# Cross attention's last group projected as rows, batch by batch, over four residual tiles

## What is computed

```python
x = _layernorm(x + _L0_attn_ref(x, ...))
x = _layernorm(x + _L0_xattn_ref(x, ctx_2048, mask, Wq, bq, Wk, bk, Wv, bv, Wo, qn_w, kn_w))
x = _layernorm(x + _L0_ffn_ref(x, ...))
...
def _L0_xattn_ref(...):
    q = _rmsnorm((x @ Wq + bq) per head, qn_w)
    k, v = the same for ctx, 4 heads, each used by 4 query heads
    probs = softmax(q @ k.T / sqrt(128) + mask)
    return (probs @ v, heads side by side) @ Wo
```

## Time and profile before

| what | value |
|---|---|
| runs | 3067.51, 3069.43, 3078.80 us; median 3069.43 |
| profiled execution | 3078.59 us, of it 3076.8 us span of the core |
| busy in that span | TensorE 2767.8 us (90%), its weight loads 2474.5 (80%), VectorE 2054.7 (67%), ScalarE 1675.5 (54%), GpSimd 1762.0 (57%) |
| TensorE clock granted over the span | 0.949 of full speed |
| chain that ended last | TensorE 24% and GpSimd 8% of the span, VectorE 7% |

### The profile page before, as it was taken

How to read it: one execution, slowest core, us unless ns; L and a number is a source line. 1 busy time by engine, 2 the same in 40 slices (tenths; PEclk the granted TensorE clock), 3 DMA queues, 4 the chain that set the end, 5 groups by cost and what they waited for, 6 DMA issues and landing times. The chain is left out here.

```text
span 3076.8 us, 48615 instructions
## 1 busy us (share of the span) xinstructions
PE 2767.8 (90%) x16114; PEld 2474.5 (80%) x16114; DVE 2054.7 (67%) x4047; ACT 1675.5 (54%) x4244; POOL 1762.0 (57%) x2193
## 2 busy tenths in 40 slices
PE   8599999968999999986799789999999996879998
PEld 7488887857888888875799688888898885769998
DVE  5377777756878888886256466767677777774334
ACT  2155555536888888863455355655656553543222
POOL 0177777734766666663245278788888786540000
PEclk9699999988999999998899899999999998889999
DMA  5635555444332333231411321211211111532101
GB/s 205 198 103 160 152 156 159 152 149 146 120 114 94 111 115 115 85 122 54 127 50 56 112 84 64 79 55 56 78 64 60 57 41 58 181 124 88 33 27 33
DMA packets 215272, 310.81 MB, mean 101 GB/s; under 512 B 47190, under 2 KB 112770, under 8 KB 212914
## 3 DMA queue, kind: packets, MB, share of 16 engines
q1 hardware_dynamic: 215026, 307.70, 31.4%
HBM read 211.27 MB, written 96.37 MB: 100 GB/s over the span
## 5 line engine op out<-in xcount | busy, mean ns | idle before, releaser
L744 POOL TENSOR_TENSOR mh_quant_d<-mh_quant_a,mh_quant_d 128x512 f32<-128x512 f32 x208 | 277.4, 1334 | 17.4
L819 ACT ACTIVATE mh_quant_d<-mh_quant_d 128x512 f32<-128x512 f32 x256 | 159.8, 624 | 109.1 <-POOL mh_quant_d L744 108.8
L738 POOL TENSOR_SCALAR mh_quant_d<-mh_quant_a 128x512 f32<-128x512 f32 x208 | 132.8, 638 | 135.2 <-DVE mh_quant_err L722 89.4
L722 DVE TENSOR_REDUCE mh_quant_err<-mh_quant_d 128x8 f32<-128x512 f32 x256 | 173.4, 678 | 37.8 <-ACT mh_quant_d L819 36.1
L1580 PE MATMUL bank<-ga_eT,ga_v 128*128 128x400 f32 (+1 forms) x384 | 169.8, 524 | 30.3 <-DVE ga_zl L1766 30.2
L2277 POOL TENSOR_TENSOR fq_var<-fq_mv,eps_ln 100x1 f32<-100x1 f32 x16 | 3.7, 229 | 314.7 <-DVE fq_mv L2220 314.7
L1537 PE MATMUL bank<-ga_xt,ga_wqh 128*128 128x400 f32 x512 | 177.3, 409 | 1.6 <-DVE ga_xt L164 1.6
L1730 ACT ACTIVATE ga_e<-ga_e,ga_nm 100x361 f32<-100x361 f32 x256 | 152.8, 597 | 38.2 <-DVE ga_nm L1825 36.7
L777 POOL TENSOR_TENSOR ga_quant_d<-ga_quant_a,ga_quant_near 128x512 f32<-128x512 f32 x128 | 165.1, 1290 | 13.4 <-DVE ga_quant_err L722 2.9
L1726 ACT ACTIVATE ga_e<-ga_e,ga_rs 100x361 f32<-100x361 f32 x256 | 152.6, 596 | 18.2 <-DVE ga_rs L1807 18.2
L1853 POOL TENSOR_TENSOR ga_qrs<-ga_qms,minus_half 100x4 f32<-100x4 f32 x64 | 68.0, 1063 | 163.5 <-DVE ga_qms L1760 163.5
(11 more groups left out here) (435 smaller groups left out, 10495.7 us busy)
## 6 DMA issues: line engine op xcount, KB each, us to landing
keys_turned<-kv_kt SPq DMA_DIRECT2D x16, 1448.0 KB, 5.8
ga_kt<-keys_turned SPq DMA_DIRECT2D x64, 362.0 KB, 2.9
ga_xt<-x_turned SPq DMA_DIRECT2D x48, 400.0 KB, 4.9
mh_xt<-x_turned SPq DMA_DIRECT2D x48, 400.0 KB, 4.8
qkv<-m_rows SPq DMA_DIRECT2D x16, 1000.0 KB
kv_rows<-qkv SPq DMA_DIRECT2D x50, 320.0 KB, 3.3
raw<-x SPq DMA_DIRECT2D x64, 200.0 KB
kv_ctx<-in_ctx SPq DMA_DIRECT2D x32, 256.0 KB, 5.2
```

What stands on the lines that cost most here:

```text
L722: nc.vector.tensor_reduce(self.of(self.err, i)[:, s, :], self.error(i, s), AX, ALU.add).then_inc(self.summed.sem, 1)
L738: nc.gpsimd.tensor_scalar(e, a[:], 1.0 / SHRINKS[s], MAGIC, ALU.mult, ALU.add).then_inc(made.sem, 1)
L744: nc.gpsimd.tensor_tensor(e, a[:], e, ALU.subtract).then_inc(self.diff.sem, 1)
L819: nc.scalar.activation(self.error(i, s), self.error(i, s), ACT.Square).then_inc(self.squared.sem, 1)
```

## The change

`project_out`, the adds to `acc` and `turn_back` are no longer done for group 15. Instead `project_rows(j)`, in slots 252, 256, 260 and 264 on TensorE, makes the rows of batch j at once: four products of `acc` (what groups 3, 7 and 11 left there) with the identity, and 12 products with the 100 tokens standing and 512 columns of Wo moving, all into one bank of its own (`row_bank`: the two query banks, the projection's bank, a score bank). The tails 12 to 15 move to slots 263 to 266, and NT becomes 269. The residual tiles are four, two of them the tiles `x` that the phase no longer needs. SyncE loads four residuals in slot 208, and afterwards the residual of e + 4 three slots behind the tail e, ahead of that slot's store. On VectorE `add_rows(e)` now comes ahead of `normalise(e - 1)`, for all 16 tails.

```diff
-        NT = NU + 24
+        NT = NU + 13
+        RES = 4
...
-        res = [sb(f"{ph}_res{n}", [S, D], F32, ctx) for n in range(2)]
+
+        res = [sb(f"{ph}_res{n}", [S, D], F32, ctx) for n in range(2)] + x
...
-        for g in range(NG):
+        for g in range(NG - 1):
             at = 0
             for n, count in enumerate(y_counts):
                 y_slots[16 * (g + 1) + 8 + n] = (g, at, at + count)
                 at += count
-        y_done = {16 * (g + 1) + 8 + n: (g, f) for g in range(NG) for f, n in enumerate((4, 6, 7, 10))}
-        tails = {16 * (g + 2) + 3 + j: 4 * (g - (NG - BG)) + j for g in range(NG - BG, NG) for j in range(G)}
+        y_done = {16 * (g + 1) + 8 + n: (g, f) for g in range(NG - 1) for f, n in enumerate((4, 6, 7, 10))}
+        tails = {16 * (g + 2) + 3 + j: 4 * (g - (NG - BG)) + j for g in range(NG - BG, NG - 1) for j in range(G)}
+        first_row = 4 * (BG - 1)
+        tails.update({NU + 7 + j: first_row + j for j in range(G)})
+        rows_at = {NU - 4 + 4 * j: j for j in range(G)}
+        row_bank = q_bank + [y_bank, score_bank[0]]
...
                 if n == NU - 48:
-                    load_res(0)
-                    load_res(1)
+                    sp.wait_ge(x_turned.sem, x_turned.upto(15))
+                    for e in range(RES):
+                        load_res(e)
+                if n - 3 in tails and tails[n - 3] + RES < 16:
+                    e = tails[n - 3]
+                    sp.wait_ge(out_in[e % RES].sem, out_in[e % RES].upto(e // RES))
+                    load_res(e + RES)
                 if n - 1 in tails:
                     e = tails[n - 1]
-                    since(sp, normed, e)
-                    sp.dma_start(rows_of(xs[2], batch(NG - BG + e // 4, e % 4)), res[e % 2][:])\
-                        .then_inc(out_in[e % 2].sem, 16)
-                    if e + 2 < 16:
-                        since(sp, out_in[e % 2], e // 2)
-                        load_res(e + 2)
+                    sp.wait_ge(normed.sem, normed.upto(e))
+                    sp.dma_start(rows_of(xs[2], batch(NG - BG + e // 4, e % 4)), res[e % RES][:])\
+                        .then_inc(out_in[e % RES].sem, 16)
...
+            def project_rows(j):
+
+                g = NG - 1
+                pe.wait_ge(y_added.sem, y_added.upto(4 * (g - BG) + 3))
+                pe.wait_ge(z_lo.sem, z_lo.upto(4 * g + j))
+                if j < 2:
+                    pe.wait_ge(q_lo.sem, q_lo.upto(GH * NG - 1))
+                elif j == 2:
+                    pe.wait_ge(y_added.sem, y_added.upto(4 * (g - 1) + 3))
+                else:
+                    pe.wait_ge(masked.sem, masked.upto(NU - 1))
+                for f in range(KC):
+                    nc.tensor.matmul(row_bank[j][0:S, f * P:(f + 1) * P], acc[groups[g][1]][:, f, cols(j)], ident[:],
+                                     start=f == 0, stop=False, skip_group_check=True)
+                for hh in range(GH):
+                    last = mm3(row_bank[j][0:S, :], zh[g % 2][:, hh, cols(j)], zl[g % 2][:, hh, cols(j)],
+                               wo[0][:, hh, :], wo[1][:, hh, :], False, hh == GH - 1)
+                last.then_inc(rows_full.sem, 1)
...
-                if n in tails:
+                if n in tails and tails[n] < first_row:
                     turn_back(tails[n])
+                if n in rows_at:
+                    project_rows(rows_at[n])
...
             def add_rows(e):
-                k = e % 2
-                since(dve, tail_turned, e)
-                since(dve, res_in[k], e // 2)
-                nc.vector.tensor_tensor(res[k][:], tail_bank[0:S, :], res[k][:], ALU.add).then_inc(added.sem, 1)
+                k, r, from_ = e % 2, res[e % RES][:], tail_bank if e < first_row else row_bank[e - first_row]
+                if e < first_row:
+                    dve.wait_ge(tail_turned.sem, tail_turned.upto(e))
+                else:
+                    dve.wait_ge(rows_full.sem, rows_full.upto(e - first_row))
+                dve.wait_ge(res_in[e % RES].sem, res_in[e % RES].upto(e // RES))
+                nc.vector.tensor_tensor(r, from_[0:S, :], r, ALU.add).then_inc(added.sem, 1)
...
+                if n in tails:
+                    add_rows(tails[n])
                 if n - 1 in tails:
                     normalise(tails[n - 1])
-                if n in tails:
-                    add_rows(tails[n])
```

More of the change, by code:

```diff
@@ L1369, in cross_attention @@
         v_in = [Signal(f"{ph}_v_in{n}", len(range(n, NQ, 3)), 32) for n in range(3)]
-        res_in, out_in = ([Signal(f"{ph}_{c}{n}", 8, 16) for n in range(2)] for c in ("res_in", "out_in"))
+        res_in, out_in = ([Signal(f"{ph}_{c}{n}", 16 // RES, 16) for n in range(RES)] for c in ("res_in", "out_in"))
         made = Signal(f"{ph}_made", 4)
@@ L1380, in cross_attention @@
         attended, z_hi, z_lo = (Signal(f"{ph}_{c}", NQ) for c in ("attended", "z_hi", "z_lo"))
-        y_full, y_added = head("y_full"), head("y_added")
-        tail_turned, added, stats_made, mv_made, eps_added, rstd_made, normed = (
-            row16(c) for c in ("tail_turned", "added", "stats", "mv", "eps_added", "rstd", "normed"))
+        y_full, y_added = (Signal(f"{ph}_{c}", 4 * (NG - 1)) for c in ("y_full", "y_added"))
+        tail_turned, rows_full = Signal(f"{ph}_tail_turned", 4 * (BG - 1)), Signal(f"{ph}_rows_full", G)
+        added, stats_made, mv_made, eps_added, rstd_made, normed = (
+            row16(c) for c in ("added", "stats", "mv", "eps_added", "rstd", "normed"))
         kview = t["L0_xattn_Wq"].rearrange("(k p) n -> p k n", p=P)
@@ L1455, in load_res @@
             def load_res(e):
-                sp.dma_start(res[e % 2][:], rows_of(xs[1], batch(NG - BG + e // 4, e % 4))).then_inc(res_in[e % 2].sem, 16)
+                sp.dma_start(res[e % RES][:], rows_of(xs[1], batch(NG - BG + e // 4, e % 4))).then_inc(res_in[e % RES].sem, 16)
             load_x(0)
@@ L1771, in add_rows @@
             def add_rows(e):
-                k = e % 2
-                since(dve, tail_turned, e)
-                since(dve, res_in[k], e // 2)
-                nc.vector.tensor_tensor(res[k][:], tail_bank[0:S, :], res[k][:], ALU.add).then_inc(added.sem, 1)
-                since(dve, added, e)
-                nc.vector.bn_stats(stats[k][:], res[k][:]).then_inc(stats_made.sem, 1)
+                k, r, from_ = e % 2, res[e % RES][:], tail_bank if e < first_row else row_bank[e - first_row]
[5 more added lines that the diff above has]
+                nc.vector.tensor_tensor(r, from_[0:S, :], r, ALU.add).then_inc(added.sem, 1)
+                dve.wait_ge(added.sem, added.upto(e))
+                nc.vector.bn_stats(stats[k][:], r).then_inc(stats_made.sem, 1)
                 since(dve, stats_made, e)
@@ L1782, in normalise @@
             def normalise(e):
-                k = e % 2
-                since(dve, rstd_made, e)
-                nc.vector.tensor_scalar(res[k][:], res[k][:], mv[k][:, 0:1], rstd[k][:], ALU.subtract, ALU.mult)\
+                k, r = e % 2, res[e % RES][:]
+                dve.wait_ge(rstd_made.sem, rstd_made.upto(e))
+                nc.vector.tensor_scalar(r, r, mv[k][:, 0:1], rstd[k][:], ALU.subtract, ALU.mult)\
                     .then_inc(normed.sem, 1)
@@ L1877, in cross_attention @@
                       scored, masked, maxed, exped, recip, scaled, turned, copied, attended, z_hi, z_lo, y_full, y_added,
-                      tail_turned, added, stats_made, mv_made, eps_added, rstd_made, normed]):
+                      tail_turned, rows_full, added, stats_made, mv_made, eps_added, rstd_made, normed]):
             s_.hand_back()
```

## The result

| | before | after |
|---|---|---|
| median, us (7 runs each, same chip) | 3076.04 (3067.51 to 3079.65) | 3063.67 (3056.16 to 3071.45) |
| ratio of the times, 95% interval | | 0.9958 (0.9944 to 0.9972) |
| profiled execution: its time, its span, us | 3078.59, 3076.8 | 3056.16, 3054.4 |
| TensorE clock granted over the span | 0.949 | 0.955 |

So 0.42% less: by the ratio 12.9 us of 3076, with an interval of 8.6 to 17.2 us. That is inside the 0.5% that count as no change here, and the median lies in the predicted range of 3047 to 3065 us. The median of before moved from 3069.43 us in three runs to 3076.04 in seven, which is why the gain ends at 3063.67 and not near 3056.

What follows compares the result with a forecast made beforehand. Latency at the end of cross attention was taken as the bound. 9.9 us at the end, 2.3 of residual waits and 2.3 by the swapped order gave 14.5 us less: median 3069.43 to 3054.9 us, range 3047 to 3065.

Steps and rivals of the forecast that it cites:

- the end: End of cross attention: the last normalisation starts at 1460.0 where it was 1469.99, so 9.9 us less.
- rival B: Last group: residuals stay late, each of four adds waits 2.36 us, gain 7.1 us, 3062.3 us; chance 0.12.
- A row costs 3.8 us: One project_rows on TensorE: 2.77 us for 12 products plus 1.0 us for the identity passes.
- the 5.8 us: Three rows on TensorE's path: extra cost if 100-column weight loads were added to the products; gain then 8.7 us.
- Rows in slots 252 and 256 are paid in full: Last units on TensorE: rows of batches 0 and 1 are not hidden and cost 7.6 us.
- Rival A: Units' end: the rows in slots 252 and 256 are hidden, 22.1 us less, 3047.3 us; chance 0.12.
- `zl` starts 5.7 us later: VectorE after the last attended batch: the last `zl` starts at 1445.0 instead of 1439.36, delayed by the rows ahead.
- `zl` to the last normalisation 15.0 us: VectorE's last group: 13.0 us of work plus 2.0 us of residual waits, where it was 30.6 us.
- the loads' waits: Residual loads of tails 13 to 15: waits of 0.7, 1.1 and 0.2 us, together 2.0 us.
- Normalisation to the next load stays at 3.06 us: Phase end: last normalisation, store and its landing, up to the next phase's first load, keep their 3.06 us.
- 2.3 us of residual waits in tails 2 to 7, and 2.3 us by the swap: VectorE beside the units: waits go with four tiles; the swapped order takes 70% of 3.3 us excess in normalisations.
- Rival C: TensorE from slot 252 on: half clock makes it slower, at worst 16 us, 3085.6 us; chance 0.10.

Runs made afterwards that it cites:

- experiment 8: The whole change with only batch 0's row early, in slot 252, the other three in slots 262 to 264; ratio to the kernel before 0.9927.
- experiments 1 and 2: Kernel before with four residual tiles alone (ratio to before 0.9976), then also with add_rows(e) ahead of normalise(e - 1) (0.9958); neither has the rows.
- experiment 4: The whole change with all four rows behind the units, in slots 261 to 264; ratio to the kernel before 0.9937.
- experiments 9 and 10: Residual loads one slot earlier in SyncE's queue, four tiles: on the whole change (ratio to before 0.9959), then with all rows behind the units (0.9927).

## Why the prediction held, and where it did not

**The size.** 14.5 us were forecast with a range of 10 to 19 for that case; 13.5 were measured in the stretch and 12.9 (8.6 to 17.2) in the times. Two pieces of luck are in this. The stretch is near the sum because two misses offset each other: the end gave 8.0 us where 9.9 were forecast, and U gave 5.5 where 4.6 were, of which about 1.8 are the clock of before. Without that clock the stretch would have gained 11.7. And the level, 3063.67 us where 3054.9 was forecast, lies in the range by 1.3 us: from the median of 3069.43, 10 to 19 us less was 3050 to 3059, and only the part of the range that reached into rival B covered the 6.6 us by which the median of before moved.

By its own steps:

- *A row costs 3.8 us*: 3.61. The products were right (2.82 for 2.77), the identity passes took 0.79 where I took 1.0. The weight loads of 100 columns (0.17 us) stayed beside the products, so the 5.8 us that the prediction priced for loads that nothing hides did not come.
- *Rows in slots 252 and 256 are paid in full*: yes for the first, 3.63 us (experiment 8); the second was not moved alone. Rival A, that both are covered, is refuted: the three rows cost 8.1 us of E.
- *`zl` starts 5.7 us later*: E grew by 5.3 us.
- *`zl` to the last normalisation 15.0 us*: 16.70. The part without loads was 13.0 in the sum and 13.14 in the kernel with eight tiles. **The failed term is the loads' waits: 2.0 us predicted, 3.29 measured.** I priced each load by the one row of 2.86 us, which had no store just ahead of it (the next one was issued 0.54 us behind it). The loads of the changed kernel are issued 0.3 us behind a store and took 3.5 to 4.0 us. In the kernel with rows alone, where each load is issued once the store of its tile has landed, the five that an add waited for in the last two groups took 2.76 to 3.01 us. The sum said 0.7, 1.1 and 0.2 us of waiting for tails 13 to 15; it was 1.15, 1.52 and 0.62, each 0.4 to 0.5 more. Rival B, 9.4 us of such waits, was far off. The 2.5 us for 200 KB, an estimate by the Trainium skill's page "DMA: Bandwidth & Descriptors" ("Anatomy of one DMA"), whose section measured it on the path of DMAs that GpSimd issues, while these are SyncE's, is further from all of these loads than the row was, and the gain that followed from it, a us more, did not come.
- *Normalisation to the next load stays at 3.06 us*: 3.69. All kernels in which the last two normalisations follow each other closely have 3.6 to 3.7 us; those with the old order 3.1 to 3.2. Two stores close together would explain it; it was not tried apart.
- *2.3 us of residual waits in tails 2 to 7, and 2.3 us by the swap*: U fell by 5.5 us in the pair of traces, of which about 1.8 are the clock of before, so 3.7 for 4.6. The part that fell short is the swap: it took 2.1 us out of the normalisations, and 1.5 us out of U (experiments 1 and 2).
- *Rival C, the clock*: granted 1.00 from 1404 to 1445 us. Nothing of it.
- *Two readings were loose*: of tails 8 to 10 only tail 10 waited for its residual. And where VectorE was busy 3.84 of 4 us, TensorE was busy all 4 at half clock, so that row alone does not show that VectorE set the pace.

**What the sum did not say.** It gave 9.9 us to "the end", and a reader would take them for the work of the rows. They are not. Rows on top of tiles and order changed E by +8.1 us (23.54 to 31.65) and N by -7.9 (24.58 to 16.70): the change's largest part gives with one hand what it takes with the other, since its first three rows stand where the units wait for TensorE. The prediction had both numbers, 11.4 us of rows on the path (5.7 of them up to `zl`) and the work removed behind `zl`, and never set one against the other alone. Doing so asks at once for the kernel of experiment 4: rows behind the last unit, in TensorE's idle time.

**Two rows to add.** The idle time of 0.39 us ahead of unit 253 and the 2.23 us of tail 10, on which the prediction rests too, are these (timeline of the kernel before):

```profile
1413.17 0.45 PE L1596 MATMUL bank<-ga_zh,ga_woh 128*128 128x400 f32 x1 [0.39 <-DVE ga_acc L1812]
...
1437.81 0.69 DVE L1775 TENSOR_TENSOR ga_res<-bank,ga_res 100x512 f32<-100x512 f32 x1 [2.23 <-DMA ga_res<-x]
```

## What to carry to other kernels

Work that is taken off a chain pays only by what it does not put back on it: cost each part of a change against the others' presence, and place new work where its engine is idle, here four calls moved for 7.8 us. Where a wait for a result, a load or a row can each be last, removing one shows the next; count what each would be alone (3.3 us for the swap without rows, 0.5 with them). Two more tiles that let a load run ahead were the cheapest edit, and more tiles did what reordering one queue could not.

## What the runs showed of the hardware that was not expected

- A 200 KB load's time from issue to use depended on what was issued just ahead of it in the same queue: 2.58 to 3.21 us when the store ahead of it had landed (14 loads, before and rows alone), 3.07 to 3.22 us when besides a store was issued 0.3 us behind the load (experiments 9 and 10), 3.51 to 4.32 us when it was issued 0.3 to 0.4 us behind a store (nine loads: after, experiments 4 and 8). The adds that end these spans all waited for the load. Whether the queue, the engines or the memory is shared was not told apart.
- The same 0.55 us normalisation on VectorE takes up to 1.54 us beside GpSimd's work on 128x512; starting it one add later took three of five such places away, without any change to GpSimd's work.
- The same program is not equally fast in the same place from one execution to the next: 16 units took 51.6 to 51.8, 52.4 to 52.6 or 53.7 us, and the self attention phase 875 to 887 us. The differences go with TensorE's granted clock: 0.97 against 0.90 over the 16 units (53.7 us, too, had 0.90), 0.96 against 0.95 over the phase. Two single profiles differ by that before any edit.
